# The row maxima of a causal attention kernel: turned by VectorE in 32x32 blocks and placed by DMA, instead of turned by TensorE and copied by ScalarE

## What is computed

```python
xn = layernorm(x) * gamma + beta
q, k, v = split(xn @ w_qkv.T)              # 16 heads of 16, q scaled by 16 ** -0.5
sim = where(causal_mask, -max_float, q @ k.T)
x = layernorm(x + softmax(sim) @ v)
h = silu(tlin(x, w1, s1)) * tlin(x, w2, s2)
h = gelu(tlin(gelu(tlin(h, h1w, h1s)), h2w, h2s))
x = layernorm(x + tlin(h, w3, s3))
```

## Time and profile before

| what | value |
| --- | --- |
| median of 3 runs | 2266.78 us (2266.12 to 2267.12) |
| profiled execution, its time | 2266.53 us |
| profiled execution, its span | 2264.9 us |
| PE, DVE, ACT, POOL busy | 99%, 76%, 72%, 10% of the span |
| granted TensorE clock, mean | 0.997 |
| attention ends, feed-forward begins | about 1610 us |

### The profile page before, as it was taken

How to read it: one execution, slowest core, us unless ns; L and a number is a source line. 1 busy time by engine, 2 the same in 40 slices (tenths; PEclk the granted TensorE clock), 3 DMA queues, 4 the chain that set the end, 5 groups by cost and what they waited for, 6 DMA issues and landing times. The chain is left out here.

```text
span 2264.9 us, 40406 instructions
## 1 busy us (share of the span) xinstructions
PE 2239.1 (99%) x15338; PEld 1244.2 (55%) x15338; DVE 1730.9 (76%) x3684; ACT 1623.4 (72%) x3087; POOL 228.3 (10%) x365
## 2 busy tenths in 40 slices
PE   8999999999999999999999999999999999999998
PEld 4444444444444445444444444443588888888887
DVE  8898998888999897888989898996535444544543
ACT  4677888899999898989989999999623433332332
POOL 3211110011110102111010211001100000000000
PEclk9999999999999999999999999999999999999999
DMA  3100001100000200000020000205500000000000
GB/s 103 34 24 17 4 20 41 38 20 20 20 20 1 59 20 20 20 20 20 1 57 20 20 20 20 78 1 168 186 10 17 3 19 19 11 9 19 16 4 20
DMA packets 72292, 70.17 MB, mean 31 GB/s; under 512 B 41632, under 2 KB 51744, under 8 KB 70688
## 3 DMA queue, kind: packets, MB, share of 16 engines
q1 hardware_dynamic: 67392, 56.03, 9.3%
q0 software_dynamic: 4704, 11.53, 1.7%
HBM read 28.20 MB, written 4.19 MB: 14 GB/s over the span
## 5 line engine op out<-in xcount | busy, mean ns | idle before, releaser
L741 ACT ACTIVATE PR<-bank 128x512 f32<-128x512 f32 (+1 forms) x2176 | 1092.6, 594 | 66.2 <-PE bank L1076 65.6
L831 DVE TENSOR_REDUCE pm<-bank 128x1 f32<-128x512 f32 x1422 | 920.3, 684 | 129.4 <-PE bank L1050 110.2
L1093 PE MATMUL bank<-PR,V 128*17 128x512 f32 (+3 forms) x4608 | 553.3, 562 | 0.5 <-POOL PR L623 0.4
L1491 PE MATMUL bank<-e_hid,e_h_sb 128*128 128x512 f32 x2048 | 466.2, 389 | 0.0
L1071 PE MATMUL bank<-MR,ones 64*128 64x512 bf16 (+3 forms) x2304 | 438.2, 369 | 1.2 <-DVE pm L834 0.7
L1491 PEld LDWEIGHTS bank<-e_hid,e_h_sb 128*128 128x128 f32 x2048 | 383.8, 188 | 81.2 <-DVE e_hid L1361 1.4
L1313 ACT ACTIVATE e_tmp<-bank,scales 128x512 f32<-128x512 f32 x128 | 88.3, 690 | 322.9 <-PE bank L1491 322.7
L726 ACT ACTIVATE mx_sb<-bank 128x512 f32<-128x512 f32 x370 | 221.3, 598 | 60.2 <-PE bank L1050 53.8
L834 DVE CUSTOM_DVE_ANT_0 bank<-bank,below 128x256 f32<-128x256 f32 (+3 forms) x512 | 239.8, 512 | 29.7 <-PE bank L1050 28.3
L1071 PEld LDWEIGHTS bank<-MR,ones 64*128 64x128 bf16 x2304 | 117.6, 93 | 250.9 <-issue 102.8
L826 DVE TENSOR_REDUCE pm<-mx_sb 128x1 f32<-128x512 f32 x370 | 250.0, 676 | 0.9 <-ACT mx_sb L726 0.8
(11 more groups left out here) (140 smaller groups left out, 1757.1 us busy)
## 6 DMA issues: line engine op xcount, KB each, us to landing
xnT<-in_h_dram SPq DMA_DIRECT2D x8, 1024.0 KB, 6.1
KA<-qk_hi SPq DMA_DIRECT2D x88, 64.0 KB, 2.2
KA<-qk_lo SPq DMA_DIRECT2D x88, 64.0 KB, 2.2
QX<-qk_hi SPq DMA_DIRECT2D x80, 64.0 KB, 2.2
QX<-qk_lo SPq DMA_DIRECT2D x80, 64.0 KB, 2.2
xres<-in_x_dram SPq DMA_DIRECT2D x8, 512.0 KB, 8.1
e_h_sb<-in_h_dram POOLq DMA_DIRECT2D x2, 2048.0 KB, 11.2
e_h_sb<-in_h_dram POOLq DMA_DIRECT2D x1, 4096.0 KB, 23.7
```

Of the source, the lines that this page charges most:

```text
L741: act.activation(PR[:, s % NPB, h, off:QB], ring_bank("score", s, h)[:, off:QB], ACT.Exp).then_inc(exp_done, 1)
L831: dve.reduce_max(pm[:, B % 2, i, a, p, 1 + c:2 + c], bank[:, :], AX.X).then_inc(mx_done, 1)
L1093: last = pe.matmul(ACC[32 * h:32 * h + VW, q:QB], V[:, v_tile(B, tile), GH * (B // NJ % 2) + h, :], PR[:, s % NPB, h, at:at + QB - q], sta ...
L1491: last = pe.matmul(RING[(4 + n) % NR][:, :], w[:, c, P * o:P * (o + 1)], hid[:, (T + layer) % 2, part, c, :], start=(c == 0 and part == 0) ...
```

## The change

The turn of the maxima leaves TensorE and ScalarE.

- `mcol` shrinks to 128 x 4 x 32: the 12 used columns of a query tile lie at 8a + 4p + part in the first 16 of 32.
- VectorE turns `mcol` (128 x 128 bf16) into `mturn` in one instruction, each 32x32 block by itself (`turn_maximum`, op "turn").
- SP then issues four DMAs (`place_maximum`), one for each 32 partitions: each takes 16 rows of `mturn`, for the four query tiles 64 bytes apiece, to the 32 columns of each tile in rows 0, 8, 16, ... 120 of `MR`. `MR` is zeroed once at the start by POOL; `ones` picks every eighth row.
- The four matmuls, their PSUM bank, the ScalarE copy and the bf16 identity go. The first score of a block waits for 64 more counts of `mrow_done`, the landing of its four DMAs.
- `ready_by(B)`: the maxima are due, and split by POOL, at `START[B] - 4`, except where the block before has only 3 steps (B = 1, 9, 17, 25), where it stays `START[B] - 3`. "turn" stands in the middle of the step behind that, among the "after" ops.
- SP's order is sorted by step: a turn counts as its step + 0.3, a `stack` as its step + 1.

```diff
-LENGTHS = {"qk": (1900, 1100), "v": (1900, 500), "maxT": (600, 500), "acc": (600, 400), "direct": (1750, 1200)}
+LENGTHS = {"qk": (1900, 1100), "v": (1900, 500), "acc": (600, 400), "direct": (1750, 1200)}
+ISSUED = {"turn": 0.3, "qk": 1}
+def ready_by(B):
+    return START[B] - MAX_AHEAD - (steps_of(B - 1) > 2 * MAX_AHEAD)
...
-            turns.setdefault(START[B] - MAX_AHEAD + 1, []).append(("maxT", B))
+            after.setdefault(ready_by(B) + 1, []).append(("turn", B))
-            last.setdefault(START[B] - MAX_AHEAD, []).append(("neg", B))
+            last.setdefault(ready_by(B), []).append(("neg", B))
...
-            due[START[item[0]] - MAX_AHEAD] = total
+            due[ready_by(item[0])] = total
...
+        def mrow_count(B):
+            return 16 * (P // BLOCK) * (B + 1)
+            def place_maximum(B):
+                sp.wait_ge(max_turned, B + 1)
+                if B >= NM:
+                    sp.wait_ge(st_ready, st_count(START[B - NM + 1] - 1, GH - 1))
+                for b in range(P // BLOCK):
+                    target = MR[0:P:P // 16, B % NM, :].rearrange("r (i b q) -> r b i q", i=TI, q=BLOCK)
+                    sp.dma_start(target[:, b, :, :], mturn[BLOCK * b:BLOCK * b + 16, :, :]).then_inc(mrow_done, 16)
+            for op in PLAN.issues:
+                if op[0] == "turn":
+                    place_maximum(op[1])
+                if op[0] == "qk":
+                    stack(op[1])
...
-                column = mcol[:, :, :].rearrange("q i (a y p s) -> q i a y p s", a=2, p=2, s=4)
+                column = mcol[:, :, 0:16].rearrange("q i (a p s) -> q i a p s", a=2, p=2, s=4)
...
-            def copy_max(B):
-                act.wait_ge(mt_ready, B + 1)
-                if B >= NM:
-                    act.wait_ge(st_ready, st_count(START[B - NM + 1] - 1, GH - 1))
-                act.activation(MR[:, B % NM, :], ring_bank("maxT", B)[:, :], ACT.Copy).then_inc(mrow_done, 1)
...
+            def turn_maximum(B):
+                dve.wait_ge(mcol_done, B + 1)
+                if B >= 1:
+                    dve.wait_ge(mrow_done, mrow_count(B - 1))
+                dve.transpose(mturn[:, :, :].rearrange("q i c -> q (i c)"),
+                              mcol[:, :, :].rearrange("q i c -> q (i c)")).then_inc(max_turned, 1)
...
-            def transpose_max(B):
-                ring_free("maxT", B)
-                pe.wait_ge(mcol_done, B + 1)
-                for i in range(TI):
-                    last = pe.matmul(ring_bank("maxT", B)[:, P * i:P * (i + 1)], mcol[:, i, :], ident_r[:, :],
-                                     start=True, stop=True)
-                last.then_inc(mt_ready, 1)
...
-                    pe.wait_ge(mrow_done, B + 1)
+                    pe.wait_ge(mrow_done, mrow_count(B))
```

More of the change, by code:

```diff
@@ L56 @@
 NEWTON = 3
-COPIED = ("norm", "qk", "v", "maxT", "acc", "acc_copy")
+COPIED = ("norm", "qk", "v", "acc", "acc_copy")
+ISSUED = {"turn": 0.3, "qk": 1}
 INTRO_QK = 2
@@ L154, in __init__, with issue_order @@
         self.relays()
+        self.issue_order()
         self.count()
+    def issue_order(self):
+        step, found = 0, []
+        for op in self.ops:
+            if op[0] == "score":
+                step = op[1]
+            if op[0] in ISSUED:
+                found.append((step + ISSUED[op[0]], op))
+        self.issues = [op for _, op in sorted(found, key=lambda f: f[0])]
     def relays(self):
@@ L254, in intro @@
         ops += first[:half] + [("direct", 1, 0)] + first[half:] + [("rowmax", 0), ("neg", 0)]
-        ops += [("stat", c) for c in range(4, NJ)] + [("direct", 1, 1), ("norm", 2), ("direct", 1, 2), ("maxT", 0),
+        ops += [("stat", c) for c in range(4, NJ)] + [("direct", 1, 1), ("norm", 2), ("direct", 1, 2), ("turn", 0),
                 ("direct", 1, 3), ("qk", 2), ("v", 0)] + second + [("inverse", 2)]
@@ L292, in count @@
         self.bank, self.former = self.take_banks()
-        self.order = {kind: [op[1] for op in self.ops if op[0] == kind] for kind in ("qk", "v", "maxT", "acc", "norm")}
-        for kind in ("qk", "v", "maxT", "acc"):
+        self.order = {kind: [op[1] for op in self.ops if op[0] == kind] for kind in ("qk", "v", "acc", "norm")}
+        for kind in ("qk", "v", "acc"):
             first = INTRO_QK if kind == "qk" else 0
@@ L370, in attend @@
         rowmax = sb("rowmax", [P, NX, TI, 2, 2])
-        mcol = sb("mcol", [P, TI, P], bf16)
+        mcol = sb("mcol", [P, TI, BLOCK], bf16)
+        mturn = sb("mturn", [P, TI, BLOCK], bf16)
         mrest = sb("mrest", [P, TI, 2, 2])
-        ident_r = sb("ident_r", [P, P], bf16)
         below = sb("below", [P, QB])
@@ L435, in attend @@
         mcol_done = sem("mcol_done")
-        mt_ready = sem("mt_ready")
+        max_turned = sem("max_turned")
         mrow_done = sem("mrow_done")
@@ L552, in _ @@
             sp.dma_start(wvg[:, 1, :, :], wv[1, :, :].rearrange("p (c f) -> p c f", c=EC)).then_inc(wg_load[1], 16)
[L553 to L557, removed]
+            def place_maximum(B):
[10 more added lines that the diff above has]
+                    stack(op[1])
+                    if op[1] % NJ == 0 and op[1] < NB - NJ:
+                        load_weights(op[1] // NJ + 1)
             sp.wait_ge(v_ready, NU)
@@ L595, in _ @@
             pool.memset(mcol[:, :, :], 0.0).then_inc(consts, 1)
+            pool.memset(MR[:, :, :], 0.0).then_inc(consts, 1)
             def split(B):
@@ L628, in split_maximum @@
                 if B >= 1:
-                    pool.wait_ge(mt_ready, B)
-                column = mcol[:, :, :].rearrange("q i (a y p s) -> q i a y p s", a=2, p=2, s=4)
-                first, second, third = (column[:, :, :, 0, :, part] for part in range(3))
+                    pool.wait_ge(max_turned, B)
+                column = mcol[:, :, 0:16].rearrange("q i (a p s) -> q i a p s", a=2, p=2, s=4)
+                first, second, third = (column[:, :, :, :, part] for part in range(3))
                 pool.tensor_copy(first, rowmax[:, B % NX, :, :, :]).then_inc(mcol_part, 1)
@@ L769, in _ @@
             act.wait_ge(const_load, 32)
-            act.wait_ge(consts, 6)
+            act.wait_ge(consts, 7)
             act.wait_ge(rows_done, 6)
@@ L782, in _ @@
                     copy_v(op[1])
-                if op[0] == "maxT":
-                    copy_max(op[1])
                 if op[0] == "unit" and op[1:] in PLAN.relay:
@@ L914, in constants @@
                 dve.wait_ge(consts, 2)
-                dve.tensor_copy(ident_r[:, :], ident[:, :]).then_inc(ones_done, 1)
-                pairs = ident[:, :].rearrange("q (a y p s) -> q p y a s", a=2, p=2, s=4)
+                pairs = ident[:, :].rearrange("q (a p s z) -> q p z a s", a=2, p=2, s=4)
                 for p in range(2):
@@ L936, in _ @@
             constants()
-            dve.wait_ge(consts, 6)
+            dve.wait_ge(consts, 7)
             for op in PLAN.ops:
@@ L948, in _ @@
                     row_maximum(op[1])
+                if op[0] == "turn":
+                    turn_maximum(op[1])
                 if op[0] == "out":
@@ L981, in ring_free @@
                     pe.wait_ge(v_done, former[1] + 1)
-                if former[0] == "maxT":
-                    pe.wait_ge(mrow_done, former[1] + 1)
                 if former[0] == "acc":
@@ L1131, in _ @@
             pe.wait_ge(consts, 2)
-            pe.wait_ge(ones_done, 3)
+            pe.wait_ge(ones_done, 2)
             pe.wait_ge(acc_zero, 1)
@@ L1148, in _ @@
                     maximum(op[1], op[2])
-                if op[0] == "maxT":
-                    transpose_max(op[1])
                 if op[0] == "score":
```

## The result

The changed kernel takes 2280.9 us (median of 4 runs, 2279.15 to 2281.23) against 2266.95 us (4 runs, 2266.12 to 2267.22) for the kernel before: 14.0 us or 0.61% slower, ratio 1.0061 with a 95% interval of 1.0043 to 1.0078. The prediction was 2270.5 us with a range of 2257 to 2278. Slower by more than 0.2% had 0.38 of its chances; the size lies outside its range.

The account below looks back on a forecast made before the run. PE, ACT and DVE, all near their limits, were taken to hold each other up through a ring of banks. Gains of 4.2 us against losses of 8.3 gave 4.1 us more, forecast 2270.5 us, range 2257 to 2278.

Parts of the forecast that it names:

- block 1 to 8: Blocks 2 to 7: VectorE's turn has no cover, charged 0.1 us each beyond the gain, 0.6 us.
- Units moved a step forward are neutral: Planned order of the attention: units due a step earlier cost nothing; the last block has one more step without units.
- The short blocks: Blocks 9, 17 and 25, behind three-step blocks: PE stalls 1.9 us each for the placed maxima, 5.7 us.
- I count it whole: Blocks 9, 17, 25: with under 2 us of ACT and DVE work in hand, the 1.9 us stall counts fully.
- The start up to block 0: Block 0's first score: placement lands at 39.8 against 39.36, 0.4 us late, of which 0.3 counted.
- lies at the start, when DVE waits for x: Zeroing of MR at the kernel's start: placed where DVE waits for x, with no cost charged.
- The placement at block 1: Block 1's first score: placement lands late, PE stalls 2.3 us, of which 1.7 us arrive at the end.
- The gain: Removed PE matmuls and ACT copy: 0.3 us a block; 4.2 us in sum after late landings eat part.
- A: All blocks: placement hidden, full gain of 9.6 to 15.4 us, 2251 to 2257 us; chance 0.22.
- B: Placement DMAs: the fourth lands at 3.3 us, not 1.8, giving 2292 us; chance 0.13.
- C: SP's queue: a stack blocks SP before a turn, one hit about 2276 us; chance 0.13 shared with D.
- D: VectorE: turn or its wait costs 0.5 us more a block, 2276 us; chance 0.13 shared with C.

Follow-up runs that it names:

- experiment 1: Changed kernel with normalising and turning of the tokens of blocks 3 to 7 back at their old steps: 2274.5 us, ratio 1.0032.
- experiment 2: Kernel before with only the changed kernel's due dates, the maxima still turned by TensorE and copied by ScalarE: 2272.1 us, ratio 1.0023.
- experiment 11: Kernel before with maxima due four steps ahead in every block, norm and scale leads at three and one steps, no exchange: 2267.8 us, ratio 1.0003.
- experiment 4: Changed kernel with POOL's zeroing of MR put behind VectorE's constants: 2279.4 us, ratio 1.0057.
- kernel of three edits: Changed kernel with old norm steps, maxima four steps ahead in all blocks, and MR zeroed behind VectorE's constants: 2263.9 us, ratio 0.9988.
- experiments 6 and 7: Kernel of three edits with a ScalarE copy put back per block, 2269.8 us, or four PE matmuls put back per block, 2267.9 us.
- experiment 8: Changed kernel with maxima due three steps ahead in all blocks and the old plan, norms at old steps too: 2366.9 us in one run.
- experiment 3: Changed kernel with maxima due four steps ahead at blocks 9, 17 and 25 too: 2270.5 us, ratio 1.0017.

## Why the prediction was off

The sum by its own terms, beside what the table of first scores gives:

| term | predicted, us | profile after, us |
| --- | --- | --- |
| up to block 0 | +0.3 | +1.9 |
| block 0 to 1 | +1.7 | +7.6 |
| block 1 to 8 | +0.6 | +1.0 (+2.9 at block 3, then -2.0) |
| around 9, 17, 25 | +5.7 | +9.5 |
| other blocks from 10 on | -4.2 | -5.3 |
| behind the attention | 0 | -0.1 (of the times; -0.3 of the spans) |
| sum | +4.1 | +14.6 |

- **The step that failed** is "Units moved a step forward are neutral". I followed the units and not what the planner hangs on them: "qk", "norm" and "scale" move too, and "norm" of block 3 came into step 0, where POOL had no time for it before PE wanted its rows, as that of block 4 into step 10. Put back, it is worth 6.4 us (experiment 1); put into the kernel before, the due dates cost 5.3 (experiment 2). It is the largest share of the missing 10.5 us. What is left of the jump between blocks 0 and 1 with the norms put back is order too: 2.6 us in experiment 11, which has no placement.
- **The short blocks** were right in mechanism and place, 2.5 us for 1.9. VectorE reached the turn 2.83 us into the step and not 2.2, because it waited 0.62 us for a bank on the way; the chain took 4.0 us and not 3.9. The second part of the error is that "I count it whole" was too little: with engines run dry and the clock at its lower level the wait of 2.5 us cost 3.1 to 3.2. Together 3.8 us.
- **The start up to block 0** had 1.9 us for 0.3. The zeroing "lies at the start, when DVE waits for x": it lay ahead of that wait, beside the constants for which PE's first matmuls wait, and cost them 0.9 us (experiment 4), costed at nothing. Against the kernel before 0.5 us of that is seen, because the bf16 identity, which VectorE made there first, is gone. Another 0.9 us is that in this execution the ten matmuls of the start were slow for longer than in the profile before. That varies between kernels that are the same up to there, so it is chance, and what the zeroing is worth in the time isn't shown. The remaining 0.5 us fits the placement, for which PE waited 1.06 us at block 0.
- **The placement at block 1** was hidden in the changed kernel by the larger loss (0.47 us of wait). With the norms back it shows: 1.41 us at block 1 in experiment 1 and 2.24 in the kernel of three edits, where the prediction had 2.3.
- **The gain** of 0.3 us a block held as a price (0.31 in experiments 6 and 7), but by another sum: I took it as PE's slot and a little of ScalarE's, and it is half the one and a third of the other. That the figures meet is partly luck. As a course it did not hold: from block 10 to 16 only 0.2 us come back, from 18 to 24 2.9, and the runs don't say why. Nor is all of the -5.3 in the table the exchange: in experiment 2, with the same due dates and no exchange, the same stretches give -2.3, so that about 3 us are its own, for the 4.2 of the prediction.
- **The rivals.** A fell: PE waited. B fell: the landing was 1.7 us, 3.1 at the most. C fell: no wait of PE for a DMA to `MR` other than the three was over 1.1 us. D fell: one wait of VectorE for POOL, 1.2 us, and a turn of 0.30 us. None of the four, and no bound of the range, had a price for a changed order near the start, which is why the range was too narrow above.
- **Two slips in the working** change nothing of this. 4.1 us on the median of 2266.78 is 2270.9, not 2270.5. And DVE as late as 495.0 gives a stall of 3.8 us by the same sum, not 3.4.

## What to carry to other kernels

When a due date moves in a planned order, list every operation that is placed relative to it, and read for each whether the engine that feeds it still has its time; a fix of three small edits to the order and the start was worth 17 us here, the exchange itself 4. A new hand-over through another engine and a DMA queue should be given its lead by the shortest step sequence and not by the usual one. Count a wait of the bounding engine at more than its length: here 1.3 times. And look at how far the untouched start of a kernel varies between profiles before a microsecond there is put down to an edit.

## What the hardware showed that I had not expected

- After PE had stood idle for 2.5 us its granted clock fell, and not at once: 1.00 during the wait, 0.66 in the 2 us in which it took up work, 0.50 in the next 2, and 0.99 behind them. By the ratio of experiment 8 such waits cost 1.3 times their length. In experiment 3 PE waited 1.28 us at block 9, and the clock stayed at 1.00 from 500 to 520 us.
- A POOL memset of 128 x 1024 bf16 (0.94 us) beside two VectorE instructions made these take 2.11 us in place of 1.22, so that it cost VectorE nearly its own length (0.89 us). The two times come back in every kernel with the zeroing at that place and without it. Which resource they share no run here shows.
- A DMA of 64-byte pieces took 0.595 us to issue and landed in 1.7 us in the median, no longer than the DMAs of 128-byte pieces in the earlier trace rows (0.601 and 1.8).
- The same ten fp32 matmuls of 128 x 512 at the start of the program took 1.06 to 1.19 us each at first and 0.59 later, and the change came after three in one execution and after six in another, with the same start at 4.50 us.
